# Ternary clipping moved from VectorE to GpSimd, constants of a count in a column of their own, keys spread over more rounds

## The chip, the cores and the metric

The kernel runs on one core of one Trainium2 chip. The metric is the device time of one execution in microseconds. The engines are TensorE (PE, its weight loads PEld), VectorE (DVE), ScalarE (ACT), GpSimd (POOL) and SyncE (SP, which here only starts transfers).

## The reference, cut to what matters

Two layers of a gated cross-attention network run one after the other. The change lies in the first attention and beside it. What is computed there:

```python
sim = einsum('bhnd,bhmd->bnm', Q, K) / (sqrt(d) * H)        # 4 x 512 x 512
topk_vals = top_k(sim, 153)[0]
threshold = topk_vals[:, :, -1:]                            # the 153rd largest of each row
A = sigmoid(sim) * (sim >= threshold)
x = x + tanh(g) * ((1 - gamma) * norm(x) + gamma * (A + A.T) * 0.5)
# the feed-forward behind it takes ternary weights:
wq = clip(round(w / mean(|w|)), -1, 1)
# the second attention needs keys made from the context: k_r = rope(ctx) @ W_kr
```

## The kernel before, in words

The threshold of each of the 2048 rows is found by bisection, without a sort. The rows lie in 16 tiles of 128 rows, and the tiles in two groups of 8 (`g` is 0 or 1). Each group takes 26 steps. A step compares every row's 512 keys (int16 numbers made from `sim`) with the row's present middle, counts those above it, and halves the interval. After 13 steps the keys are made anew at a finer scale (`refine`, line 744). The list `EVENTS` orders the 52 steps as rounds k = 0 to 51: rounds 0 to 3 and then every odd round up to 47 are of group 0, every even round from 4 on and the last four are of group 1, so that one group is counted while the other is marked.

A round goes like this:

- `mark(k)` on VectorE writes marks (0 or 1) for 5 or 6 of the 8 tiles (line 771), and `marks(k)` on ScalarE writes signs for the other 3 or 2 (line 591). In odd rounds from 15 to 41 VectorE has 5 tiles, in all others 6. Both wait for the group's new middles (`mid`). VectorE signals `md`, ScalarE `ma`.
- `total(k)` on TensorE adds the marks up: 32 products with the identity (line 444), each of 8 blocks of 16 columns, collect 128 partial sums (8 tiles by 16) in the group's PSUM bank. Ahead of them stands one product (line 441) that puts the constants `less` under the sums; it waits for VectorE's marks only.
- `count` on VectorE adds each tile's 16 partial sums (line 777) and `halve` makes the new middle (line 782). VectorE does this after the marks of the following round, so its order is mark(k+1), count(k), halve(k), mark(k+2).

Other work is woven into the rounds. After `total(k)`, TensorE makes the products of keys that `keys_made(k)` lists (line 478, an fp32 product of 128 x 512 into banks 2 to 5). VectorE copies a key out two rounds later when the round's number is divisible by 3 (line 867), ScalarE in the other rounds (line 614), and SyncE sends it to memory. ScalarE scales and rounds one of 12 pieces of ternary weights to int16 (`scaled`, line 558) in the rounds `SCALED` = 15, 17, 20, 22, 25, 27, 30, 32, 35, 37, 40, 42. VectorE clips it to -1..1 and writes bf16 (`ternary`, line 759) two rounds later, after that round's marks and the halving. The clipping frees one of three ring buffers; SyncE then loads the next piece (line 377). GpSimd turns the context (`krot`, up to 39 us) and makes the factors `xa` and `xb` (up to 86.5 us); then it has nothing to do until 217.6 us.

The clipping's place in an iteration of VectorE's loop over the rounds:

```python
mark(k)
if held:
    count(*held)
    halve(*held)
    held = None
if k - 2 in SCALED:
    ternary(SCALED.index(k - 2))
```

Of the kernel before, what the change touches and what calls it, by code (L numbers as in the profile page):

```python
# [20 lines left out]
TOPK = 153  # L21
# [6 lines left out]
NW = 12  # L28
# [194 lines left out]
class Front:  # L223


    def __init__(self, M, K):
        self.nm = Norms(M)
        self.ctxt = M.tile([128, 4, S], F32, "ctxt")
        self.wqk = M.tile([128, 2, 128], F32, "wqk")
        self.qt = M.tile([128, 2, S], F32, "QT")  # L230
        self.kt = M.tile([128, 2, S], F32, "KT")
        self.sim = M.tile([128, NT, S], F32, "SIM")
        self.a2 = [M.tile([128, 4, S], F32, "A2")]
        M.top += 8192
        at = M.top
        self.a2.append(M.tile([128, 4, S], F32, "A2b"))
        M.top = at
        self.ring = [M.tile([128, 2048], F32, f"wr{i}") for i in range(3)]
        self.wsum = M.tile([128, NW], F32, "wsum")
        self.wmsum = M.tile([128, 4], F32, "wmsum")  # L240
        self.winv = M.tile([128, 4], F32, "winv")
        self.center = M.tile([128, NT], F32, "center")
        self.unit = M.tile([128, NT], F32, "unit")
        self.shift = M.tile([128, NT], F32, "shift")
        self.base = M.tile([128, NT], F32, "base")
        self.dense = M.tile([128, 2, NT], F32, "dense")
        self.mid = M.tile([128, NT], F32, "mid")
        self.cnt = M.tile([128, NT], F32, "cnt")
        self.cb = M.tile([128, NT], F32, "cb")
        self.xa = M.tile([128, NT], F32, "xa")  # L250
        self.xb = M.tile([128, NT], F32, "xb")
        self.marks = M.tile([128, NT, S], BF16, "marks")
        self.less = M.tile([128, 2, 8, 16], BF16, "less")
        self.stt = M.tile([128, NT, 6], F32, "sst")
        self.smv = M.tile([128, NT, 2], F32, "smv")
        self.sd = M.tile([128, NT], F32, "sd")

        at = M.top
        M.top = M.at["WG"] + 20480
        first = M.tile([128, 4, S], I16, "KEYa")  # L260
        M.top = M.at["WG"] + 28672
        second = M.tile([128, 4, S], I16, "KEYb")
        M.top = M.at["QT"]
        fine = M.tile([128, 8, S], I16, "KEYc")
        M.top = M.at["A2"] + 8192
        self.other = M.tile([128, 8, S], I16, "KEYd")
        M.top = at
        self.coarse, self.fine = (first, second), fine

        M.top = M.at["A2"]  # L270
        self.kvt = M.tile([128, 4, S], F32, "KVT")
        self.kts = M.tile([128, 4, S], F32, "KTS")
        M.top = M.at["WD"]
        self.ktab = M.tile([128, 2, S], F32, "KTAB")
        self.wkr = M.tile([128, NH // 2, 128], F32, "WKR")
        self.kst = M.tile([128, 4, S], F32, "KST")
# [30 lines left out]
SCALED = [15 + 5 * i // 2 for i in range(NW)]  # L307


def on_vector(k):  # L310

    return LEAST if SCALED[0] <= k < SCALED[-1] and k % 2 else LEAST + 1
# [7 lines left out]

def keys_before(k):

    return min(32, max(0, k - KEYS_FROM) + sum(j < k for j in (9, 12, 15, 18)))


def keys_made(k):
# [86 lines left out]
def front_tensor(e, w, K, F0):  # L413
# [22 lines left out]
    def total(k):  # L436

        g, it = EVENTS[k]
        w.wait_ge(S_["less"], 8)
        w.wait_ge(S_[f"md{g}"], it + 1)  # L440
        e.matmul(PS[7 - g][:, 0:128], K.identb[:], F.less[:, on_vector(k) - LEAST].rearrange("p t c -> p (t c)"), start=True, stop=False)
        w.wait_ge(S_[f"ma{g}"], it + 2)
        for c in range(32):
            m = e.matmul(PS[7 - g][:, 0:128], K.identb[:], F.marks[:, 8 * g:8 * g + 8, 16 * c:16 * c + 16], start=False, stop=c == 31)  # L444
        m.then_inc(S_[f"total{g}"].sem, 1)

    def similar(tiles):
# [235 lines left out]
def front_vector(e, w, dc, K, F0):  # L683
# [3 lines left out]
    e.memset(K.magic[:], MAGIC).then_inc(S_["const"].sem, 1)  # L687


    dc.inc(e.memset(F.less[:], 0.0))  # L690
    w.wait_ge(dc.sem, dc.n)
    for i in range(2):
        e.memset(F.less[:, i, 0:LEAST + i, 0], -352.0).then_inc(S_["less"].sem, 1)
        e.memset(F.less[:, i, 0:LEAST + i, 1], 352 - (512 - TOPK + 0.5)).then_inc(S_["less"].sem, 1)
        e.memset(F.less[:, i, LEAST + i:8, 0], -200.0).then_inc(S_["less"].sem, 1)
        e.memset(F.less[:, i, LEAST + i:8, 1], 200 - (512 - 2 * TOPK + 1.5)).then_inc(S_["less"].sem, 1)
    w.wait_ge(S_["d_cst"], 16)
    dc.inc(e.tensor_copy(K.identb[:], K.ident))
    for k in range(4):
# [47 lines left out]
        dc.inc(m)  # L747
        w.wait_ge(dc.sem, dc.n)

    def ternary(i):  # L750

        r = rounded(F, i)
        w.wait_ge(S_["wsc"], i + 1)
        if i >= 8:
            w.wait_ge(S_["kmm"], 32)
            for j in range(4):
                w.wait_ge(S_[f"d_st{j}"], 128)
        w.wait_ge(S_["ma0"], COARSE + 1 if i in (6, 7) else 0)
        e.tensor_scalar(wtile(K, i), r.rearrange("p (a n) -> p a n", a=4) if i >= 8 else r, -1.0, 1.0, ALU.max, ALU.min).then_inc(S_["wq"].sem, 1)

    def mark(k):

        g, it = EVENTS[k]
# [10 lines left out]
    def count(g, it):  # L774
        c = slice(8 * g, 8 * g + 8)
        w.wait_ge(S_[f"total{g}"], it + 1)
        dc.inc(e.tensor_reduce(F.cnt[:, c], PS[7 - g][:, 0:128].rearrange("p (t c) -> p t c", t=8), AX, ALU.add))

    def halve(g, it):
        c = slice(8 * g, 8 * g + 8)  # L780
# [41 lines left out]
    for k, (g, it) in enumerate(EVENTS[:LATE + 4]):  # L822
        mark(k)
        if held:
            count(*held)
            halve(*held)
            held = None
        if k - 2 in SCALED:
            ternary(SCALED.index(k - 2))
        late = k - LATE  # L830
        if k == 0:
            w.wait_ge(S_["gth"], 2)
            dc.inc(e.tensor_scalar(K.cc[:, 2:3], K.gth[:, 0:1], -0.5, 0.5, ALU.mult, ALU.add))
            w.wait_ge(dc.sem, dc.n)
            dc.inc(e.tensor_tensor(K.cc[:, 0:1], K.cc[:, 2:3], K.gth[:, 1:2], ALU.mult))
            dc.inc(e.tensor_scalar(K.cc[:, 3:4], K.gth[:, 0:1], 0.25, 0.25, ALU.mult, ALU.add))
            w.wait_ge(dc.sem, dc.n)
            e.tensor_tensor(K.cc[:, 1:2], K.cc[:, 3:4], K.gth[:, 1:2], ALU.mult).then_inc(S_["cc"].sem, 1)
        elif k == 12:
            w.wait_ge(S_["wabs"], NW)  # L840
            for m in range(3):
                e.tensor_reduce(F.wmsum[:, m:m + 1], F.wsum[:, 4 * m:4 * m + 4], AX, ALU.add).then_inc(S_["wmsum"].sem, 1)
        elif k == 16:
            feed_factors(e, w, dc, K, F0)
        elif k == 14:
            w.wait_ge(S_["wtot"], 1)
            for m in range(3):
                dc.inc(e.tensor_scalar(K.G0[:, m:m + 1], PS[0][:, m:m + 1], 1.0 / (1 << 20), EPS, ALU.mult, ALU.max))
            w.wait_ge(dc.sem, dc.n)
            e.reciprocal(F.winv[:, 0:3], K.G0[:, 0:3]).then_inc(S_["winv"].sem, 1)  # L850
        elif late in (0, 1):
            kept(*range(4 * late, 4 * late + 4))
        elif late == 2:
            back(0, 1, 2, 3)
        elif late == 3:
            feed0_stats(e, w, dc, K, F0)
        if k in ROWS:
            rows(range(2 * ROWS.index(k), 2 * ROWS.index(k) + 2))
        for t in SPREAD.get(k, ()):
            spread(t)  # L860
        if k == LEAD - 1:
            bounds(1)
        for i in keys_out(k) if key_on_vector(k) else ():
            w.wait_ge(S_["kmm"], i + 1)
            w.wait_ge(S_[f"d_st{i % 4}"], 16 * (i // 4))
            w.wait_ge(S_["kev"], i)
            e.tensor_copy(F.kst[:, i % 4], PS[2 + i % 4][:]).then_inc(S_["kev"].sem, 1)
        held = g, it
        if k == len(EVENTS) - 1 or EVENTS[k + 1][0] == g:
            count(g, it)  # L870
            halve(g, it)
            held = None
# [43 lines left out]
def front_gpsimd(e, w, pc, K):  # L916

    S_, F = K.S, K.F
    for b in range(4):
        w.wait_ge(S_["d_ktab"], 16)  # L920
        w.wait_ge(S_[f"d_ctx{b}"], 16)
        w.wait_ge(S_[f"d_kts{b}"], 16)

        w.wait_ge(S_["md0"], 1 if b == 3 else 0)
        e.tensor_tensor(F.kvt[:, b], F.ctxt[:, b], F.ktab[:, 0], ALU.mult)
        w.wait_ge(S_["md0"], 2 if b == 3 else 0)
        pc.inc(e.tensor_tensor(F.kts[:, b], F.kts[:, b], F.ktab[:, 1], ALU.mult))
        w.wait_ge(S_["md0"], 3 if b == 3 else 0)
        w.wait_ge(pc.sem, pc.n)
        e.tensor_tensor(F.kvt[:, b], F.kvt[:, b], F.kts[:, b], ALU.add).then_inc(S_["krot"].sem, 1)  # L930
# [9 lines left out]
    pc.inc(e.tensor_scalar(F.xb[:], F.xb[:], -1.0, None, ALU.mult))  # L940
    w.wait_ge(pc.sem, pc.n)
    e.tensor_scalar(F.xa[:], F.xa[:], 1.0, None, ALU.add).then_inc(S_["cb"].sem, 1)


def front_done(w, K):
# [2365 lines left out]
```

## Time and profile before

| what | us |
|---|---|
| median of 3 runs | 1734.05 (1732.85 to 1735.21) |
| the profiled execution, its own time | 1732.34 |
| its span in the trace | 1730.5 |
| rounds 0 to 51, first mark to last count | 24.0 to 209.4 |

The span is the time between the first and the last instruction of the trace; 1.8 us of the execution lie around it. Durations below are of this one execution. In the timeline a row may merge several instructions of one line that follow each other; the number after x is their count.

### The profile page before, as it was taken

To read this page: it belongs to the slowest core of one execution; us is meant where nothing else is said; L and a number is where in the kernel's file an instruction comes from. 1 tells how busy PE (TensorE), PEld (TensorE's weight loads), DVE (VectorE), ACT (ScalarE), POOL (GpSimd) and SP (SyncE) were. 2 spreads that over 40 slices of the span, in tenths; PEclk is the share of its full clock that TensorE was granted. 3 is DMA by queue.
4 is the path that set the end of the run, shared out by engine and by line. 5 is a ranking of instruction groups with operands and counts; after the bars stand their busy time and mean duration, and the time that the engine had idled before them with its cause. 6 is when DMAs were issued, how large, how long until landed. Compare 5 with 4: busy or idle time off the path is not lost.

```text
span 1730.5 us, 28004 instructions
## 1 busy us (share of the span) xinstructions
PE 1662.8 (96%) x9726; PEld 1174.6 (68%) x9776; DVE 1501.7 (87%) x2933; ACT 1019.8 (59%) x1863; POOL 811.7 (47%) x876
## 2 busy tenths in 40 slices
PE   8798899999998999999999899999999999999999
PEld 5576766666665666676666578778777877874443
DVE  6988889999998899999999887877887888879885
ACT  7888778879996212112111766666666665646664
POOL 3100023121222777666666677667666666755110
PEclk9999999999999999999999999999999999999999
DMA  8764116556751233223333523323223223133444
GB/s 323 265 214 166 38 51 158 125 122 165 163 133 37 74 108 81 82 73 81 81 79 107 174 70 88 88 70 92 77 70 87 81 62 80 50 124 75 92 90 106
DMA packets 157915, 186.05 MB, mean 108 GB/s; under 512 B 85584, under 2 KB 112464, under 8 KB 154576
## 3 DMA queue, kind: packets, MB, share of 16 engines
q1 hardware_dynamic: 146160, 154.58, 32.6%
q10 hardware_dynamic: 11616, 29.70, 6.1%
q8 instruction: 78, 1.28, 0.3%
q14 instruction: 61, 0.50, 0.1%
HBM read 110.83 MB, written 37.75 MB: 86 GB/s over the span
## 4 chain that ended last, share of the span: by engine, by line
PE 69%; DVE 22%; ACT 4%; issue 3%; POOL 1%; DMA 0%; ACTq 0%; DVEq 0%
PE ps L2613 6%; PE ps L2602 5%; PE ps L2103 4%; PE ps L2682 4%; PE ps L2736 3%; PE ps L2738 3%; PE ps L2737 3%; PE ps L444 3%; PE ps L2684 3%; PE ps L2683 3%; PE ps L2058 3%; PE ps L1646 3%; PE ps L1664 3%; PE ps L2060 3%; PE ps L1638 3%
## 5 line engine op out<-in xcount | busy, mean ns | idle before, releaser
L2652 POOL TENSOR_SCALAR E<-E,ri 128x512 f32<-128x512 f32 x250 | 387.0, 1565 | 188.2 <-DVE ri L2636 177.8
L2622 ACT ACTIVATE E<-ps,nm 128x512 f32<-128x512 f32 x256 | 175.5, 691 | 85.4 <-DVE nm L2629 85.4
L2371 POOL TENSOR_TENSOR R<-R,R 128x512 f32<-128x512 f32 x128 | 163.1, 1296 | 115.1 <-DVE R L2312 115.1
L2754 ACT ACTIVATE TH<-ps 128x512 fp32r<-128x512 f32 x256 | 140.0, 602 | 123.3 <-PE ps L2613 123.3
L2823 DVE TENSOR_TENSOR TL<-ps,TH 128x512 fp32r<-128x512 f32 x256 | 165.2, 685 | 29.0 <-ACT TH L2754 28.7
L2191 ACT ACTIVATE KH<-ps 128x512 fp32r<-128x512 f32 x64 | 38.3, 598 | 247.1 <-PE ps L2083 232.3
L2629 DVE TENSOR_REDUCE nm<-ps 128x1 f32<-128x512 f32 x256 | 162.3, 679 | 0.5 <-PE ps L2602 0.4
L1575 POOL TENSOR_SCALAR sc<-sc,gs 128x1 f32<-128x1 f32 x32 | 15.0, 468 | 310.0 <-DVE sc L1447 310.0
L2613 PE MATMUL ps<-CST,E 128*128 128x128 f32 x1024 | 134.2, 273 | 3.0 <-DVE TL L2823 1.5
L2613 PEld LDWEIGHTS ps<-CST,E 128*128 128x128 f32 x1024 | 118.8, 140 | 24.9 <-issue 3.6
L1438 DVE SCALAR_TENSOR_TENSOR U<-fTH,sc,ps 128x512 f32<-128x512 f32 x128 | 95.1, 745 | 27.7 <-PE ps L1646 19.0
L2682 PE MATMUL ps<-TH,VH 128*128 128x512 f32 x256 | 110.9, 433 | 0.0
L2602 PE MATMUL ps<-KP,QR 64*128 64x512 f32 x384 | 106.4, 409 | 2.5 <-DVE R L2313 2.5
L444 PE MATMUL ps<-marks,identb 128*128 128x128 bf16 x1664 | 105.9, 224 | 2.1 <-ACT marks L591 1.8
L2602 PE MATMUL ps<-KS,QR 64*128 64x512 f32 x384 | 106.5, 409 | 0.0
L444 PEld LDWEIGHTS ps<-marks,identb 128*128 128x128 bf16 x1664 | 99.3, 101 | 9.3 <-issue 5.4
L2058 PE MATMUL ps<-HH,WQH 128*128 128x512 f32 x256 | 103.8, 405 | 0.0
L2684 PE MATMUL ps<-TH,VL 128*128 128x512 f32 x256 | 101.3, 396 | 0.0
L2736 PE MATMUL ps<-MH,CH 128*128 128x512 f32 x256 | 100.2, 391 | 0.8 <-DVE X L2832 0.8
L2683 PE MATMUL ps<-TL,VH 128*128 128x512 f32 x256 | 100.6, 393 | 0.0
L2060 PE MATMUL ps<-HH,WQL 128*128 128x512 f32 x256 | 100.1, 391 | 0.0
L2738 PE MATMUL ps<-MH,CL 128*128 128x512 f32 x256 | 99.9, 390 | 0.0
(294 smaller groups left out, 4515.7 us busy)
## 6 DMA issues: line engine op xcount, KB each, us to landing
wr<-in_wff SPq DMA_DIRECT2D x24, 1024.0 KB, 5.4
aw<-in_wff ACTq DMA_DIRECT2D x40, 512.0 KB, 4.8
scratch<-QS SPq DMA_DIRECT2D x128, 128.0 KB, 2.4
KS<-KP SPq DMA_DIRECT2D x64, 256.0 KB, 3.6
QR<-scratch SPq DMA_DIRECT2D x64, 256.0 KB, 3.4
keys<-KST SPq DMA_DIRECT2D x32, 256.0 KB, 3.2
KR<-keys SPq DMA_DIRECT2D x30, 256.0 KB, 3.8
wscr<-awb ACTq DMA_DIRECT2D x24, 256.0 KB, 3.4
```

Of the source, the lines that this page charges most:

```text
L444: m = e.matmul(PS[7 - g][:, 0:128], K.identb[:], F.marks[:, 8 * g:8 * g + 8, 16 * c:16 * c + 16], start=False, stop=c == 31)
L2058: e.matmul(key_bank(K, n)[:], wh, Q.hh[:, b, k, :], start=k == 0, stop=False)
L2371: e.tensor_tensor(Q.r1[:, z, c, :], Q.r1[:, z, c, :], ask_r2(Q, n)[:, c, :], ALU.add).then_inc(S_["radd"].sem, 1)
L2602: m = e.matmul(K.PS[2 * z + u][:], queries(A, n)[r, a, c], k[u][r, p % 2, b, :], start=i == 0, stop=i == 2)
L2613: m = e.transpose(K.PS[4 + x % 2][:, 128 * c:128 * c + 128], A.e[:, x % EB, 128 * c:128 * c + 128], K.ident)
L2622: e.activation(A.e[:, x % EB, :], K.PS[x % 4][:], ACT.Exp, bias=A.nm[:, c], accum_out=A.sm[:, c]).then_inc(S_["exp"].sem, 1)
L2629: e.tensor_reduce(A.nm[:, c], K.PS[x % 4][:], AX, ALU.max, negate=True).then_inc(S_["mx"].sem, 1)
L2652: e.tensor_scalar(A.e[:, x % EB, :], A.e[:, x % EB, :], A.ri[:, x % 8:x % 8 + 1], None, ALU.mult).then_inc(K.S["pl"].sem, 1)
L2682: e.matmul(PS[6][:], vh, A.th[:, n % 2, c, :], start=c == 0, stop=False)
L2683: e.matmul(PS[6][:], vh, A.tl[n % 2][:, c, :], start=False, stop=False)
L2684: m = e.matmul(PS[6][:], vl, A.th[:, n % 2, c, :], start=False, stop=c == 3)
L2823: e.tensor_tensor(A.tl[n % 2][:, :, c], PS[4 + x % 2][:].rearrange("p (c n) -> p c n", c=4), A.th[:, n % 2, :, c].bitcast(F32), ALU.subtra ...
```

## The change

- The constants leave the 128 partial sums. Each tile's sums now have 17 columns in PSUM (`counts`, 8 blocks at a pitch of 17): 16 for the marks and one for the constants. Two products of 8 columns write the constant column in a group's first round and again when the number of VectorE's tiles differs from the round two before; the 32 products of marks overwrite their own 16 columns each round. `count` adds 17 columns. A clearing of `less` at the start goes.
- The keys: exactly one product of keys a round, in rounds 4 to 35. Before, rounds 9, 12, 15 and 18 made two, and the last was in round 31.
- The clipping moves from VectorE's rounds to GpSimd, all 12 behind `xa`. GpSimd starts each as soon as ScalarE has rounded the piece and the place of its output is free. The two bounds are applied in the other order.

```diff
--- before.py
+++ after.py
@@ -250,7 +250,7 @@
         self.xa = M.tile([128, NT], F32, "xa")
         self.xb = M.tile([128, NT], F32, "xb")
         self.marks = M.tile([128, NT, S], BF16, "marks")
-        self.less = M.tile([128, 2, 8, 16], BF16, "less")
+        self.less = M.tile([128, 2, 2, 8], BF16, "less")
         self.stt = M.tile([128, NT, 6], F32, "sst")
         self.smv = M.tile([128, NT, 2], F32, "smv")
         self.sd = M.tile([128, NT], F32, "sd")
@@ -307,6 +307,11 @@
 SCALED = [15 + 5 * i // 2 for i in range(NW)]
 
 
+def counts(K, g):
+
+    return K.PS[7 - g][:, 0:136].rearrange("p (t c) -> p t c", t=8)
+
+
 def on_vector(k):
 
     return LEAST if SCALED[0] <= k < SCALED[-1] and k % 2 else LEAST + 1
@@ -320,7 +325,7 @@
 
 def keys_before(k):
 
-    return min(32, max(0, k - KEYS_FROM) + sum(j < k for j in (9, 12, 15, 18)))
+    return min(32, max(0, k - KEYS_FROM))
 
 
 def keys_made(k):
@@ -438,10 +443,12 @@
         g, it = EVENTS[k]
         w.wait_ge(S_["less"], 8)
         w.wait_ge(S_[f"md{g}"], it + 1)
-        e.matmul(PS[7 - g][:, 0:128], K.identb[:], F.less[:, on_vector(k) - LEAST].rearrange("p t c -> p (t c)"), start=True, stop=False)
+        if it == 0 or on_vector(k) != on_vector(k - 2):
+            for i in range(2):
+                e.matmul(counts(K, g)[:, :, 16], K.identb[:], F.less[:, on_vector(k) - LEAST, i], start=i == 0, stop=i == 1)
         w.wait_ge(S_[f"ma{g}"], it + 2)
         for c in range(32):
-            m = e.matmul(PS[7 - g][:, 0:128], K.identb[:], F.marks[:, 8 * g:8 * g + 8, 16 * c:16 * c + 16], start=False, stop=c == 31)
+            m = e.matmul(counts(K, g)[:, :, 0:16], K.identb[:], F.marks[:, 8 * g:8 * g + 8, 16 * c:16 * c + 16], start=c == 0, stop=c == 31)
         m.then_inc(S_[f"total{g}"].sem, 1)
 
     def similar(tiles):
@@ -687,13 +694,11 @@
     e.memset(K.magic[:], MAGIC).then_inc(S_["const"].sem, 1)
 
 
-    dc.inc(e.memset(F.less[:], 0.0))
-    w.wait_ge(dc.sem, dc.n)
     for i in range(2):
-        e.memset(F.less[:, i, 0:LEAST + i, 0], -352.0).then_inc(S_["less"].sem, 1)
-        e.memset(F.less[:, i, 0:LEAST + i, 1], 352 - (512 - TOPK + 0.5)).then_inc(S_["less"].sem, 1)
-        e.memset(F.less[:, i, LEAST + i:8, 0], -200.0).then_inc(S_["less"].sem, 1)
-        e.memset(F.less[:, i, LEAST + i:8, 1], 200 - (512 - 2 * TOPK + 1.5)).then_inc(S_["less"].sem, 1)
+        e.memset(F.less[:, i, 0, 0:LEAST + i], -352.0).then_inc(S_["less"].sem, 1)
+        e.memset(F.less[:, i, 1, 0:LEAST + i], 352 - (512 - TOPK + 0.5)).then_inc(S_["less"].sem, 1)
+        e.memset(F.less[:, i, 0, LEAST + i:8], -200.0).then_inc(S_["less"].sem, 1)
+        e.memset(F.less[:, i, 1, LEAST + i:8], 200 - (512 - 2 * TOPK + 1.5)).then_inc(S_["less"].sem, 1)
     w.wait_ge(S_["d_cst"], 16)
     dc.inc(e.tensor_copy(K.identb[:], K.ident))
     for k in range(4):
@@ -747,17 +752,6 @@
         dc.inc(m)
         w.wait_ge(dc.sem, dc.n)
 
-    def ternary(i):
-
-        r = rounded(F, i)
-        w.wait_ge(S_["wsc"], i + 1)
-        if i >= 8:
-            w.wait_ge(S_["kmm"], 32)
-            for j in range(4):
-                w.wait_ge(S_[f"d_st{j}"], 128)
-        w.wait_ge(S_["ma0"], COARSE + 1 if i in (6, 7) else 0)
-        e.tensor_scalar(wtile(K, i), r.rearrange("p (a n) -> p a n", a=4) if i >= 8 else r, -1.0, 1.0, ALU.max, ALU.min).then_inc(S_["wq"].sem, 1)
-
     def mark(k):
 
         g, it = EVENTS[k]
@@ -774,7 +768,7 @@
     def count(g, it):
         c = slice(8 * g, 8 * g + 8)
         w.wait_ge(S_[f"total{g}"], it + 1)
-        dc.inc(e.tensor_reduce(F.cnt[:, c], PS[7 - g][:, 0:128].rearrange("p (t c) -> p t c", t=8), AX, ALU.add))
+        dc.inc(e.tensor_reduce(F.cnt[:, c], counts(K, g), AX, ALU.add))
 
     def halve(g, it):
         c = slice(8 * g, 8 * g + 8)
@@ -825,8 +819,6 @@
             count(*held)
             halve(*held)
             held = None
-        if k - 2 in SCALED:
-            ternary(SCALED.index(k - 2))
         late = k - LATE
         if k == 0:
             w.wait_ge(S_["gth"], 2)
@@ -916,6 +908,21 @@
 def front_gpsimd(e, w, pc, K):
 
     S_, F = K.S, K.F
+
+    def ternary(i):
+
+        r = rounded(F, i)
+        w.wait_ge(S_["wsc"], i + 1)
+        if i == 8:
+            w.wait_ge(S_["krot"], 4)
+        elif i > 8:
+            w.wait_ge(S_["kmm"], 32)
+        if i > 9:
+            for j in range(4):
+                w.wait_ge(S_[f"d_st{j}"], 128)
+        w.wait_ge(S_["ma0"], COARSE + 1 if i in (6, 7) else 0)
+        e.tensor_scalar(wtile(K, i), r.rearrange("p (a n) -> p a n", a=4) if i >= 8 else r, 1.0, -1.0, ALU.min, ALU.max).then_inc(S_["wq"].sem, 1)
+
     for b in range(4):
         w.wait_ge(S_["d_ktab"], 16)
         w.wait_ge(S_[f"d_ctx{b}"], 16)
@@ -940,6 +947,8 @@
     pc.inc(e.tensor_scalar(F.xb[:], F.xb[:], -1.0, None, ALU.mult))
     w.wait_ge(pc.sem, pc.n)
     e.tensor_scalar(F.xa[:], F.xa[:], 1.0, None, ALU.add).then_inc(S_["cb"].sem, 1)
+    for i in range(NW):
+        ternary(i)
 
 
 def front_done(w, K):
```

## Rows read from the trace of the kernel before

**Rows 1.** Page, part 1: busy us (share), instructions.
```profile
PE 1662.8 (96%) x9726; PEld 1174.6 (68%) x9776; DVE 1501.7 (87%) x2933; ACT 1019.8 (59%) x1863; POOL 811.7 (47%) x876
```

**Rows 2.** Busy time in stretches: us, PE, PEld, DVE, ACT, POOL, PEclk, DMA, GB/s.
```profile
84.00:112.00 28.00, 28.00 (x336) 21.45 (x335) 22.85 (x96) 26.25 (x35) 1.99 (x7) 1.00 0.72 250
...
152.00:183.00 31.00, 25.17 (x409) 23.17 (x407) 28.10 (x112) 25.82 (x33) 0.00 (x0) 1.00 0.33 116
```

**Rows 3.** Waits, 84 to 183 us: us in total, times, longest.
```profile
DVE cnt L777 <- PE ps L444: 12.5, 18, 1.6
```

**Rows 4.** Counts of VectorE, 84 to 183 us: ns min/median/max, starts.
```profile
L777 DVE TENSOR_REDUCE cnt<-ps x33: 279/291/293, 83.8 to 182.8; 128x8 f32<-128x128 f32 x33
```

**Rows 5.** Timeline, 92 to 100 us: start, us, engine, line, operation.
```profile
92.15 1.94 PE L478 MATMUL ps<-KVT,WKR 128*128 128x512 f32 x4
92.33 0.57 ACT L614 ACTIVATE KST<-ps 128x512 f32<-128x512 f32 x1
...
96.37 0.69 DVE L759 TENSOR_SCALAR WG<-wr 128x2048 bf16<-128x2048 int16 x1
...
96.68 0.22 PE L441 MATMUL ps<-less,identb 128*128 128x128 bf16 x1
...
96.73 1.95 PE L444 MATMUL ps<-marks,identb 128*128 128x128 bf16 x32
96.97 0.35 DVE L771 TENSOR_SCALAR marks<-KEYd,mid 128x512 bf16<-128x512 int16 x1
...
97.31 1.40 DVE L771 TENSOR_SCALAR marks<-KEYd,mid 128x512 bf16<-128x512 int16 x5
...
98.52 1.08 PE L478 MATMUL ps<-KVT,WKR 128*128 128x512 f32 x2
```

**Rows 6.** Timeline, 157 to 161 us.
```profile
157.40 1.99 ACT L558 ACTIVATE wr<-wr,winv 128x2048 int16<-128x2048 f32 x1
157.41 0.28 DVE L777 TENSOR_REDUCE cnt<-ps 128x8 f32<-128x128 f32 x1
...
157.93 0.35 DVE L771 TENSOR_SCALAR marks<-KEYd,mid 128x512 bf16<-128x512 int16 x1
...
159.30 1.32 ACT L591 ACTIVATE marks<-KEYd,mid 128x512 bf16<-128x512 int16 x2
...
160.67 1.96 PE L444 MATMUL ps<-marks,identb 128*128 128x128 bf16 x32 [0.71 <-ACT marks L591]
```

**Rows 7.** Timeline, 19 to 29 us, VectorE beside GpSimd.
```profile
19.62 1.26 POOL L930 TENSOR_TENSOR KVT<-KVT,KTS 128x512 f32<-128x512 f32 x1
...
27.98 1.11 DVE L838 TENSOR_TENSOR cc<-cc,gth 128x1 f32<-128x1 f32 x1
```

**Rows 8.** VectorE's line 717: ns min/median/max, first and last start.
```profile
L717 DVE TENSOR_SCALAR sd<-smv x2: 172/628/1083, 19.8 to 43.5; 128x8 f32<-128x8 f32 x2
```

**Rows 9.** Timeline, 79 to 84 us, marks beside small GpSimd work.
```profile
79.50 1.47 DVE L771 TENSOR_SCALAR marks<-KEYd,mid 128x512 bf16<-128x512 int16 x5
...
80.31 0.22 POOL L111 TENSOR_TENSOR bna<-bna,bnve 128x16 f32<-128x16 f32 x1
...
82.61 1.32 POOL L109 TENSOR_TENSOR bna<-bnr 128x16 f32<-128x16 f32 x1
...
83.25 0.60 DVE L771 TENSOR_SCALAR marks<-KEYb,mid 128x512 bf16<-128x512 int16 x2
```

**Rows 10.** GpSimd's groups by shape: busy us, mean ns, idle before.
```profile
L2652 POOL TENSOR_SCALAR E<-E,ri 128x512 f32<-128x512 f32 x250 | 387.0, 1565 | 188.2 <-DVE ri L2636 177.8 <-ACT E L2645 10.4
...
L113 POOL TENSOR_SCALAR G<-G 128x4 f32<-128x4 f32 x12 | 2.4, 199 | 1.0
...
L113 POOL TENSOR_SCALAR bna<-bna 128x16 f32<-128x16 f32 x3 | 0.6, 205 | 0.3
...
L942 POOL TENSOR_SCALAR xa<-xa 128x16 f32<-128x16 f32 x1 | 0.3, 270 | 0.1
```

**Rows 11.** Timeline, 117 us: a count after a pause of TensorE.
```profile
117.50 3.62 PE L444 MATMUL ps<-marks,identb 128*128 128x128 bf16 x32
```

## The prediction

> **What bounds the kernel now.** I read the page's busy times first. TensorE is busy for 96% of the span and VectorE for 87% [rows 1], but that is a mean over stages, and this change touches only the rounds, 24 to 209 us. So I read the busy times of stretches. From 84 to 112 us TensorE is busy without a gap and VectorE for 22.85 of 28 us; from 152 to 183 us TensorE has 25.17 of 31 us and VectorE 28.10 [rows 2]. So two regimes follow each other. While keys are made TensorE sets the pace, and when the keys are done VectorE (with ScalarE) does.
>
> The waits between 84 and 183 us say how often. 33 counts start there [rows 4], and before 18 of them VectorE stood still for TensorE's sums, 12.5 us in all or 0.69 us each [rows 3]. Those 0.69 us are slack of VectorE. The other 15 were late through VectorE or ScalarE themselves. ScalarE's signs in their turn wait for the new middles, so whatever delays VectorE's halving delays ScalarE.
>
> The timeline shows a round of each kind. At 96.73 us a count begins on TensorE (1.95 us), and one key follows at 98.52. Round 15 has two keys: x4 records in 1.94 us against x2 in 1.08, so one key costs TensorE 0.86 us [rows 5]. At 157.40 us ScalarE rounds a piece for 1.99 us, its signs of the next round come at 159.30 for 1.32, and TensorE's sums start only behind them at 160.67 [rows 6]. There ScalarE binds, and work taken from VectorE gives nothing.
>
> **The constants.** Each round loses one product of 128 columns of the 33. A round's 32 take 1.95 us and one alone (line 441) 0.22, so they follow each other at (1.95 - 0.22)/31 = 0.056 us [rows 5]. Where VectorE is late nothing hides it either, since the product stands between the last mark and the sums. I take 30 rounds by 0.056 = -1.7 us, bounds 0 and 52 x 0.056 = -2.9. The products of constants that remain (two in each of four rounds) and 8 more columns a count are not in the trace; below nothing they can't be, and from the 0.056 us of a 16 times wider product they are under 0.5 us together. I take +0.2. The clearing at the start lies before the first DMA has landed and costs nothing.
>
> **The keys.** Three doubles (rounds 12, 15, 18) lie where TensorE sets the pace: 3 x 0.86 = -2.6 us. Round 9's lies where VectorE is late. The four go to rounds 32 to 35, where TensorE has some room and ScalarE has little. I charge 0.86 once for TensorE there, and ScalarE copies three of these four keys, 0.57 us each [rows 5], in rounds 34, 35 and 37, next to its roundings; half of 1.7 is on the path. Sum -2.6 + 0.9 + 0.8 = -0.9 us; bounds -2.6 and +0.8. SyncE's four later stores of keys are read only in a much later stage.
>
> **The clip off VectorE.** It starts at 96.37 us and takes 0.69, and the next mark begins at 96.97, 0.60 behind its start [rows 5]. Two of the 12 lie beside the remaking of keys, where VectorE alone is at work: 2 x 0.60. Of the other ten, four are followed by a wait for TensorE or lie where ScalarE binds as at 160.67, and give nothing. Six I count at half, 0.3. Sum -3.0 us; bounds 0 and 12 x 0.60 = -7.2.
>
> **The clip on GpSimd** is not in the trace. Two numbers are wanted: its length, and what it does to VectorE.
>
> Length: multiplying 128 x 512 by a number per row takes GpSimd 1565 ns [rows 10], or 2.67 ns an element over a base of 0.2, which makes 0.2 + 2048 x 2.67 = 5.7 us. But that row and line 942 (270 ns for 16 elements) have one operation and none behind it. Line 113 has two operations with constants, as the clip has. It takes 199 ns for 4 elements and 205 for 16 [rows 10], 0.5 ns an element, or 1.2 us for 2048. The clip is nearest to line 113 in form. Such small rows show little of a slope, so I take twice theirs, 1 ns: 2.2 us, of which some 2.0 behind the start-up of 0.2. Bounds 1.2 and 5.7.
>
> Effect: at 19.62 us GpSimd works for 1.26 us, and a VectorE instruction that starts at 19.8 takes 1.083, to the end of GpSimd's, where its twin at 43.5 takes 0.172 [rows 7, 8]. L838 takes 1.11 us for one column beside GpSimd's next run [rows 7]. So some instructions of VectorE stand still while GpSimd works. Are the marks among them? At 82.61 a GpSimd instruction of 16 columns takes 1.32 us instead of 0.2 and ends when the run of marks ends (83.25 + 0.60) [rows 9]. At 79.50 five marks take 1.47 us instead of the 1.40 of another round [rows 5], beside GpSimd instructions of 0.22 us that were not held up [rows 9]. So marks and GpSimd do exclude each other, and GpSimd can slip in between two marks. The first row speaks for an exclusion for a whole instruction, the second for one that costs only what is really moved.
>
> The Trainium skill has a rule here (SBUF — State Buffer, Who interferes with whom): VectorE's two-port modes, which tensor_scalar enters, and GpSimd share one pair of ports, and whoever is first keeps it for its whole instruction. By it the sum would be the one I make below; by the row at 79.50 alone the clips would cost nothing, and the change would save 5.4 us. The Trainium skill's GPSIMD Engine Reference, 4.1 Engine selection, calls one-input work there roughly line-rate; at 1 element a cycle of its 1.2 GHz that is an estimate of 1.7 us for 2048, which the 1565 ns for 512 contradict and line 113 does not.
>
> I take the whole instruction, because L717 and L838 waited for all of it. A clip starts when ScalarE's rounding ends, at any point of VectorE's round. If it slips in between marks, the marks end 2.0 us later. If it waits for the end of the marks, 0.52 us of counting and halving would have passed anyway (from the count at 157.41 to the marks at 157.93, 0.52) [rows 6], though the halving itself reads two tensors like L838 and waits; then the next marks are 1.5 us late. Mean 1.74. Six clips (after the roundings of rounds 15, 17, 20, 25, 32 and 40) fall where TensorE sets the pace and 0.69 us is free: 6 x 1.05 = 6.3. Six fall where nothing is free: 6 x 1.74 = 10.4. Sum +16.7 us. With 1.0 in place of 2.0 it is 6 x 0.04 + 6 x 0.73 = +4.6; with 5.5 it is 6 x 4.54 + 6 x 5.23 = +58.6. Behind the delayed marks stand TensorE's sums, the count, and ScalarE's signs. GpSimd itself delays nobody: its next work is at 217 us, and a clip of 2.2 us ends before VectorE's did (two rounds later), so the ring loads come earlier, not later.
>
> **Sum.** -1.7 + 0.2 - 0.9 - 3.0 + 16.7 = +11.3 us. The stage behind the rounds starts from the last count, so it moves as a whole. The profiled execution took 1732.34 us (span 1730.5 and 1.8 around it), which makes 1743.6. It lies 1.7 us below the median of the runs, so for the median I add to 1734.05: 1745.4 us. A difference under 0.2%, 3.5 us, can't be told from none here.
>
> **Rivals.**
> - *The clips cost VectorE nothing* (the row at 79.50, for example because GpSimd takes its ports piece by piece): -5.4 us, 1728.7, faster. Against it stand L717 and L838. The turning point is 5.4/12 = 0.45 us of delay per clip. Chance 0.24.
> - *Short holds*: a clip of 1.2 us. -5.4 + 4.6 = -0.8, 1733.3, no change. Chance 0.12 with what lies around it.
> - *A slow clip*, 5.7 us, as line 2652's rate has it: -5.4 + 58.6 = +53 us. TensorE then stands still for some 4 us each time, and at 117.50, after such a pause, 32 products took 3.62 us instead of 1.95 [rows 11]: up to 12 x 1.67 = 20 us more. 1787 to 1807. For it: the only long tensor_scalar rows of GpSimd. Chance 0.14.
> - *Sums at a pitch of 17 columns slow TensorE down.* No row has such an output. With 1/8 more a product, 32 x 0.007 = 0.22 us a round; over 50 rounds +11 us, on top. The nearest row for an upper bound is a key's 0.86 us for 2 x 512 columns, 0.84 ns a column against 0.44 now: 1.6 us in each of the 35 or so rounds where TensorE is the pace or nearly, +57 us. The Trainium skill (PSUM — Partial Sum Buffer, Specifications (TRN2)) says that any non-contiguous access slows matmuls significantly, without a figure. The marks are read in blocks of 16 already, without harm. Chance that this decides: 0.06.
>
> **How the numbers follow.** The forecast case has the remaining 0.44, with its own range of 1738 to 1763 (clip of 1.4 to 3.7 us). The likeliest time is 1745.4. The range must reach to the faster rival and leave out the slow clip: 1728 to 1772. Faster 0.24, same 0.12, slower 0.64.
>
> **What would show it.** Right: in the rounds from 15 on, marks (line 771) or halvings beside a GpSimd clip of 2 us or more have maxima of 1 to 2 us instead of the 0.35 at 96.97, the waits of TensorE for marks grow, and a round with a clip is about 1.4 us longer. A round paced by TensorE should get 0.056 us shorter, and rounds 12, 15 and 18 by 0.86. Wrong: marks of 0.35 us beside the clips (the faster rival), a clip far from 2.2 us, or spacings of marks' products above 0.056 us.

## Result and the profile after

The changed kernel takes 1744.93 us (median of 6 runs, 1742.15 to 1746.65), the kernel before in the same series 1734.34 us (1732.69 to 1735.47). The ratio is 1.0058, 95% interval 1.0048 to 1.0069: slower, by some 10 us. The forecast was 1745.4 us. The profiled execution took 1742.8 us, with a span of 1741.0, or 10.5 us more than before.

The page, part 1, busy us of each engine, as in [rows 1]:

```profile
PE 1668.1 (96%) x9682; PEld 1179.0 (68%) x9732; DVE 1514.1 (87%) x2921; ACT 1018.9 (59%) x1862; POOL 834.3 (48%) x888
```

GpSimd has 22.6 us and 12 instructions more. VectorE lost 12 clips and its busy time still rose by 12.4 us. The busy times of stretches answer to [rows 2] (us, PE, PEld, DVE, ACT, POOL, PEclk, DMA, GB/s):

```profile
84.00:112.00 28.00, 26.73 (x328) 20.87 (x327) 25.28 (x95) 24.56 (x32) 7.67 (x10) 1.00 0.62 210
152.00:183.00 31.00, 25.88 (x361) 21.97 (x360) 28.94 (x94) 26.00 (x34) 7.85 (x5) 1.00 0.43 149
```

From 84 to 112 us TensorE no longer works without a gap, and VectorE went from 22.85 to 25.28 us. From 152 to 183 us VectorE is busy for 28.94 us with 94 instructions where it had 28.10 with 112: fewer instructions, each longer. Which ones is seen in VectorE's groups by shape from 84 to 193 us (busy us, mean ns of one | idle before). First the kernel before:

```profile
L771 DVE TENSOR_SCALAR marks<-KEYd,mid 128x512 bf16<-128x512 int16 x108 | 31.3, 349 | 0.3
...
L771 DVE TENSOR_SCALAR marks<-KEYc,mid 128x512 bf16<-128x512 int16 x68 | 19.9, 348 | 0.2
...
L782 DVE SCALAR_TENSOR_TENSOR mid<-cnt,base 128x8 f32<-128x8 f32 x36 | 6.0, 167 | 1.2
L759 DVE TENSOR_SCALAR WG<-wr 128x2048 bf16<-128x2048 int16 x8 | 5.5, 689 | 0.1
...
L744 DVE TENSOR_SCALAR KEYc<-SIM,center,dense 128x512 int16<-128x512 f32 x8 | 3.7, 546 | 0.1
```

And the changed kernel:

```profile
L765 DVE TENSOR_SCALAR marks<-KEYd,mid 128x512 bf16<-128x512 int16 x102 | 34.5, 397 | 0.5
L765 DVE TENSOR_SCALAR marks<-KEYc,mid 128x512 bf16<-128x512 int16 x64 | 23.7, 424 | 0.4
L776 DVE SCALAR_TENSOR_TENSOR mid<-cnt,base 128x8 f32<-128x8 f32 x34 | 11.1, 326 | 1.2
...
L749 DVE TENSOR_SCALAR KEYc<-SIM,center,dense 128x512 int16<-128x512 f32 x8 | 5.3, 734 | 0.1
```

Count times rise of the mean: 102 x 0.048 + 64 x 0.076 + 34 x 0.159 + 8 x 0.188 = 16.7 us, or 1.4 us for each of the 12 clips. I call this sum the hold. The twelve clips that left VectorE were worth 12 x 0.69 = 8.3 us of its time. The medians did not move; single instructions did. Duration by line (ns min/median/max), 84 to 193 us, of the marks, the halving, the clip and TensorE's sums:

```profile
L765 DVE TENSOR_SCALAR marks<-KEYd,mid x102: 337/347/2045, 84.3 to 191.4; 128x512 bf16<-128x512 int16 x102
...
L776 DVE SCALAR_TENSOR_TENSOR mid<-cnt,base x34: 166/168/1795, 84.1 to 192.3; 128x8 f32<-128x8 f32 x34
...
L924 POOL TENSOR_SCALAR WG<-wr x8: 1892/1892/2076, 90.5 to 152.7; 128x2048 bf16<-128x2048 int16 x8
...
L451 PE MATMUL ps<-marks,identb x1065: 219/226/327, 84.0 to 193.0; 128*128 128x128 bf16 x178
```

The same line of marks had a maximum of 383 ns before, the halving 169. The clip takes 1892 ns. And TensorE's product of marks has a median of 226 ns; before it was 219 (the line stands under the experiment with a pitch of 18). The timeline from 90 us on shows single cases (start, us, engine, line), beside [rows 5]:

```profile
90.27 3.09 DVE L765 TENSOR_SCALAR marks<-KEYd,mid 128x512 bf16<-128x512 int16 x5
...
90.54 1.89 POOL L924 TENSOR_SCALAR WG<-wr 128x2048 bf16<-128x2048 int16 x1 [4.00 <-ACT wr L565]
...
93.42 2.07 PE L451 MATMUL ps<-marks,identb 128*128 128x128 bf16 x32 [0.81 <-DVE marks L765]
...
96.23 2.06 PE L451 MATMUL ps<-marks,identb 128*128 128x128 bf16 x32
...
98.21 1.89 POOL L924 TENSOR_SCALAR WG<-wr 128x2048 bf16<-128x2048 int16 x1 [5.78 <-ACT wr L565]
...
98.66 1.46 DVE L776 SCALAR_TENSOR_TENSOR mid<-cnt,base 128x8 f32<-128x8 f32 x1
```

Five marks take 3.09 us in place of 1.40, since a clip begins at 90.54 behind the first of them; TensorE's sums then wait. At 98.66 the halving ends at 100.12, with the clip (98.21 + 1.89 = 100.10). That is what L717 and L838 did in [rows 7, 8]. The waits of the changed kernel, 84 to 193 us (us in total, times, longest), answer to [rows 3], which end at 183:

```profile
ACT marks L598 <- DVE mid L776: 23.1, 20, 2.8
...
PEld ps L451 <- DVE marks L765: 20.3, 14, 5.3
PE ps L451 <- DVE marks L765: 12.8, 6, 4.5
...
DVE cnt L771 <- PE ps L451: 7.7, 13, 1.6
```

In the same 84 to 193 us of the kernel before, VectorE waits for TensorE 20 times, 13.1 us in all, where it now does so 13 times and for 7.7 us. TensorE's waits for VectorE's marks grow from 10.7 us to 14.6 (the 12.8 above and 1.8 of line 448). The last count of the 52 starts 7.1 us later. First the kernel before, then the changed one (ns min/median/max, first and last start):

```profile
L777 DVE TENSOR_REDUCE cnt<-ps x52: 258/291/293, 30.6 to 209.1; 128x8 f32<-128x128 f32 x52
```
```profile
L771 DVE TENSOR_REDUCE cnt<-ps x52: 267/299/301, 30.4 to 216.2; 128x8 f32<-128x136 f32 x52
```

So 7.1 of the 10.5 us arise in the rounds. Another 1.8 arise directly behind them: the feed-forward's first product with the weights WG (line 1195 before, 1204 after; below the first gate product) starts at 222.9 and 231.9 us, 9.0 us apart. There the first products of the feed-forward ran at a lower granted clock. The stretches from 210 us on, first of the kernel before:

```profile
210.00:222.00 12.00, 6.70 (x28) 4.72 (x27) 8.49 (x23) 7.42 (x12) 0.59 (x2) 0.87 0.07 27
222.00:234.00 12.00, 11.93 (x57) 6.29 (x58) 9.66 (x18) 9.47 (x16) 0.57 (x2) 0.99 0.00 1
```

and of the changed kernel:

```profile
210.00:222.00 12.00, 8.87 (x68) 5.88 (x66) 9.86 (x35) 7.78 (x14) 0.00 (x0) 0.95 0.13 44
222.00:234.00 12.00, 9.82 (x34) 6.59 (x34) 6.64 (x12) 7.07 (x11) 0.59 (x2) 0.62 0.00 0
```

The same work lies 7 us later in the changed kernel, so the four rows have to be read together. At the lower of the two clock levels (1.2 GHz, a clock of 0.5) TensorE spent some 3.4 of the 24 us before, and 10.3 of them after. The remainder, 1.5 us, comes in later stages, which the change doesn't touch. Some of it may be the clock again: from 960 to 980 us the granted clock is 0.91 in the changed kernel's execution and 1.00 in the other.

### The profile page after: what moved, and what is told of

Its sections match the earlier page's. It is cut to its first block, busy times and chain, and to the rows that moved or that the text cites. A ratio compares the mean times of both kernels' runs of the same rounds, so it can differ in the third digit from the quotient of the medians.

```text
span 1741.0 us, 27965 instructions
## 1 busy us (share of the span) xinstructions
PE 1668.1 (96%) x9682; PEld 1179.0 (68%) x9732; DVE 1514.1 (87%) x2921; ACT 1018.9 (59%) x1862; POOL 834.3 (48%) x888
## 4 chain that ended last, share of the span: by engine, by line
PE 67%; DVE 23%; ACT 4%; issue 3%; POOL 1%; DMA 0%; ACTq 0%; SPq 0%; DVEq 0%
PE ps L2622 6%; PE ps L2611 5%; PE ps L2112 4%; PE ps L2691 4%; PE ps L2745 3%; PE ps L2747 3%; PE ps L2746 3%; PE ps L451 3%; PE ps L2693 3%; PE ps L2692 3%; PE ps L1655 3%; PE ps L1673 3%; PE ps L2067 3%; PE ps L1647 3%; PE ps L2069 3%
## 5 line engine op out<-in xcount | busy, mean ns | idle before, releaser
L2661 POOL TENSOR_SCALAR E<-E,ri 128x512 f32<-128x512 f32 x250 | 387.0, 1565 | 188.9 <-DVE ri L2645 177.8
L2380 POOL TENSOR_TENSOR R<-R,R 128x512 f32<-128x512 f32 x128 | 162.5, 1292 | 117.3 <-DVE R L2321 117.3
L451 PEld LDWEIGHTS ps<-marks,identb 128*128 128x128 bf16 x1664 | 104.4, 103 | 52.7 <-DVE marks L765 40.0
L451 PE MATMUL ps<-marks,identb 128*128 128x128 bf16 x1664 | 111.7, 231 | 26.2 <-DVE marks L765 21.3
```

What stands on the lines that cost most here:

```text
L451: m = e.matmul(counts(K, g)[:, :, 0:16], K.identb[:], F.marks[:, 8 * g:8 * g + 8, 16 * c:16 * c + 16], start=c == 0, stop=c == 31)
L2380: e.tensor_tensor(Q.r1[:, z, c, :], Q.r1[:, z, c, :], ask_r2(Q, n)[:, c, :], ALU.add).then_inc(S_["radd"].sem, 1)
L2661: e.tensor_scalar(A.e[:, x % EB, :], A.e[:, x % EB, :], A.ri[:, x % 8:x % 8 + 1], None, ALU.mult).then_inc(K.S["pl"].sem, 1)
```

## Experiments

Executions of one kernel differ in their mean granted clock, and the time goes with it: over all executions of this study a fit gives 1.06 us for 0.001 of mean clock. The last column is each kernel's time by that fit at a clock of 0.993, where the kernel before has 1733.3 ± 0.4. It is a help against the scatter and no more: where an edit itself makes TensorE pause and its clock fall, that column takes part of the edit's own cost away. The kernel before ran again beside each group of experiments: its median is 1733.46 beside the first four and 1731.92 beside the others.

| kernel | median us | ratio to before, 95% | last count starts | at equal clock |
|---|---|---|---|---|
| changed | 1744.93 | 1.0058 [1.0048, 1.0069] | 216.2 | 1742.7 ± 1.1 |
| clip only | 1741.10 | 1.0054 [1.0039, 1.0068] | 216.7 | 1741.4 ± 1.0 |
| constants only | 1737.83 | 1.0032 [1.0017, 1.0047] | 209.4 | 1737.1 ± 1.0 |
| keys only | 1734.82 | 1.0008 [0.9996, 1.0020] | 211.0 | 1734.0 ± 0.7 |
| all but the clip | 1738.38 | 1.0037 [1.0023, 1.0050] | 211.8 | 1735.9 ± 0.9 |
| constants, column outer | 2003.59 | 1.1562 [1.1546, 1.1578] | | |
| constants, pitch 18 | 1733.31 | 1.0005 [0.9996, 1.0014] | 204.4 | 1733.6 ± 0.8 |
| changed, clip twice | 1766.34 | 1.0197 [1.0181, 1.0212] | 243.1 | 1760.4 ± 1.6 |
| changed, clip in four | 1737.71 | 1.0032 [1.0019, 1.0044] | 210.3 | 1737.4 ± 1.1 |

The last count is that of one profiled execution each. How much of a difference there is the edit's own is seen where it arises. The start of some counts, read from the timelines, in us; for all but the first column, the difference to it:

| | before | clip only | constants | pitch 18 | keys only | all but clip | changed | in four |
|---|---|---|---|---|---|---|---|---|
| round 0 | 30.6 | -0.9 | -0.4 | -0.5 | +0.2 | -1.0 | -0.2 | -0.3 |
| round 22 | 117.3 | +1.6 | +0.7 | -1.2 | -2.2 | -3.1 | +0.8 | -0.7 |
| round 25 | 127.8 | +2.1 | -0.3 | -4.2 | -2.0 | -4.3 | -0.2 | -3.3 |
| round 36 | 162.7 | +5.0 | -0.2 | -4.5 | -1.4 | -2.1 | +4.0 | -0.5 |
| round 38 | 167.7 | +5.8 | -0.2 | -4.5 | +2.0 | +2.3 | +4.9 | 0.0 |
| round 51 | 209.1 | +7.6 | +0.4 | -4.7 | +2.0 | +2.8 | +7.1 | +1.2 |
| first gate product | 222.9 | +7.4 | +2.9 | -3.3 | +2.9 | +5.3 | +9.0 | +1.4 |
| granted clock, 112 to 137 us | 0.86 | 0.86 | 0.93 | 1.00 | 0.86 | 0.93 | 0.93 | 1.00 |

Between rounds 22 and 25 the difference follows the last row and not the edit: at a clock of 0.86 it moves by 0.5 us at most, at 0.93 by -1.0 to -1.2, at 1.00 by -2.6 and -3.0. So up to 3 us of a last count can be this alone.

**Clip only.** The kernel before, with `ternary` and its 12 calls on GpSimd as in the change.

```diff
-        if k - 2 in SCALED:
-            ternary(SCALED.index(k - 2))
+    for i in range(NW):      # in front_gpsimd, behind xa
+        ternary(i)
```

> The kernel before with the clipping alone moved to GpSimd. Theory A (a clip of 1.9 us keeps VectorE's marks and halvings out for its whole length): 12 holds of some 1.7 us less the free time where TensorE sets the pace, less 3 us of clipping that leaves VectorE: +9 to +14 us against before, nearly the whole effect of the change, with marks of up to 1.9 us in the trace. Theory B (the sums at a pitch of 17 columns, 2.06 us instead of 1.95 a round, carry the loss): below +5 us.

Measured 1.0054, most of the whole change's loss. The hold, summed as above over all of VectorE's groups, is 18.1 us here (16.8 in the changed kernel). 18.1 less the 8.3 us of the clips taken away is 9.8; the time rose by 8.1 ± 1.1. That is 1 to 1.5 us below what theory A expected and well above theory B. So the free clip is out: GpSimd holds VectorE, and most of the hold reaches the end.

**Constants only.** `counts`, the column of constants, `less` and the count of 17 columns as in the change; clips and keys as before.

```diff
-    return K.PS[7 - g][:, 0:128]
+    return K.PS[7 - g][:, 0:136].rearrange("p (t c) -> p t c", t=8)
```

> The kernel before with the constants alone in a column of their own (pitch of 17). Theory A: a round paced by TensorE gains 0.056 us by the missing product and loses 0.11 by slower ones, so 0 to +3 us against before. Theory B: +5 us or more.

Measured 1.0032, slower, where the prediction had a gain of 1.5 us. The 32 products of marks take 2.06 us instead of 1.95: (2.06 - 1.95) = 0.11 us more a round against 0.056 us for the product that fell away. The time lies between the two theories' ranges, and 33 to 50 rounds of the difference of 0.055 us are only 1.8 to 2.8 us.

**Keys only.**

```diff
-    return min(32, max(0, k - KEYS_FROM) + sum(j < k for j in (9, 12, 15, 18)))
+    return min(32, max(0, k - KEYS_FROM))
```

> The kernel before with one product of keys in each of rounds 4 to 35 alone. The prediction's term: -0.9 us, bounds -2.6 and +0.8. A rival: the four late keys meet ScalarE's roundings and the change is +1 us or more.

Measured 1.0008, no difference that can be told, where -0.9 was forecast. The timeline of this kernel shows a wait that the prediction lacked:

```profile
163.84 0.69 DVE L759 TENSOR_SCALAR WD<-wr 128x2048 bf16<-128x2048 int16 x1 [2.04 <-DMA keys<-KST]
...
166.24 0.29 PE L441 MATMUL ps<-less,identb 128*128 128x128 bf16 x1 [3.11 <-DVE marks L771]
...
166.32 3.27 PE L444 MATMUL ps<-marks,identb 128*128 128x128 bf16 x32
```

The last four clips write where the keys' staging lies, so `ternary` waits for all 32 keys and the landing of their stores. With keys up to round 35 the ninth clip stands still for that store for 2.04 us on VectorE, with the marks of the round queued behind it, and TensorE waits 3.11 us. Behind that pause its 32 products take 3.27 us instead of 1.95; from 166 to 170 us its granted clock is 0.62. By the table above the whole costs 3.4 us (from -1.4 in round 36 to +2.0 in round 38), after the keys had gained 2.4 us up to round 22.

**All but the clip.** Constants and keys as in the change, clips on VectorE.

```diff
-    for i in range(NW):      # GpSimd, of the changed kernel
-        ternary(i)
+        if k - 2 in SCALED:  # VectorE, as before
+            ternary(SCALED.index(k - 2))
```

> The changed kernel with the clipping back on VectorE, so constants and keys together. Theory A: -2 to +2 us against before. Theory B: +5 us or more. If the parts add up, it is the sum of the two runs with one part each.

Measured 1.0037, between the two theories' ranges as it stands (4.9 us). At equal clock it is 6.8 ± 1.4 us below the changed kernel: that is the clip's share when the rest is in place. The kernel is 2.6 us above the kernel before at equal clock, where the two parts sum to 3.8 + 0.7 = 4.5. The wait for the keys' store is here too, in the waits of VectorE from 150 to 200 us:

```profile
DVE cnt L782 <- PE ps L451: 5.1, 8, 2.0
DVE WD L764 <- DMA keys<-KST: 2.6, 1, 2.6
```

In the changed kernel VectorE has no such line, and GpSimd's clips wait only for ScalarE's rounding.

**Constants, column outer.** To make TensorE's output contiguous again, column c of tile t at 8c + t; TensorE then reads the marks with 512 elements between neighbours.

```diff
-            m = e.matmul(counts(K, g)[:, :, 0:16], K.identb[:], F.marks[:, 8 * g:8 * g + 8, 16 * c:16 * c + 16], ...
+            m = e.matmul(counts(K, g)[:, 0:16, :], K.identb[:], F.marks[:, 8 * g:8 * g + 8, 16 * c:16 * c + 16].rearrange("p t c -> p c t"), ...
```

> The constants-only kernel, but with the 17 columns of a tile strewn (column c of tile t at 8c + t), so that a product writes 128 neighbouring PSUM columns and reads its marks at a large step instead. If the pitch of 17 in PSUM is what made 32 products take 2.06 us in place of 1.95, they take 1.95 again and a round paced by TensorE gains 0.056 us: 0 to -2 us against before at an equal clock. If the gaps are innocent, or reading at a step is the slower side, products take 2.06 us or more and the kernel is +3 us or more.

Measured 1.156. TensorE is busy for all of 92 to 152 us at a granted clock of 0.54, and 32 products take 7.18 us, 3.7 times the 1.95. The clock accounts for a factor of up to 1.9, so the read accounts for another 2 or so. It says nothing on the output's pitch; for that it was the wrong experiment, since it moved the step to the side where it costs far more. Why the clock stays low while TensorE is busy throughout is open.

**Constants, pitch 18.** The blocks of sums 18 columns apart, an even number; the count reads 17 of them.

```diff
-    return K.PS[7 - g][:, 0:136].rearrange("p (t c) -> p t c", t=8)
+    return K.PS[7 - g][:, 0:144].rearrange("p (t c) -> p t c", t=8)
...
-        dc.inc(e.tensor_reduce(F.cnt[:, c], counts(K, g), AX, ALU.add))
+        dc.inc(e.tensor_reduce(F.cnt[:, c], counts(K, g)[:, :, 0:17], AX, ALU.add))
```

> The constants-only kernel with a pitch of 18 columns in place of 17 (every tile's sums begin on an even column). If an odd start is what slows the products, they fall back to 1.95 us for 32 and the kernel is 3 to 4 us faster than constants-only. If any gap in the output costs, they stay at 2.06 and the time too.

Measured 1.0005: the loss is gone, 3.5 ± 1.3 us at equal clock. The product of marks by line (ns min/median/max), 84 to 193 us, first before, then pitch 17 (constants only), then pitch 18:

```profile
L444 PE MATMUL ps<-marks,identb x1137: 217/219/314, 84.8 to 193.0; 128*128 128x128 bf16 x190
```
```profile
L451 PE MATMUL ps<-marks,identb x1132: 219/226/327, 84.6 to 192.9; 128*128 128x128 bf16 x189
```
```profile
L451 PE MATMUL ps<-marks,identb x1175: 216/219/315, 84.0 to 193.0; 128*128 128x128 bf16 x196
```

At a pitch of 18 the output has gaps too, so gaps as such cost nothing. What costs is the pitch of 17, at which every second block starts on an odd column; no other odd pitch was measured. In the rounds the two profiled executions part by 5.1 us (+0.4 and -4.7), of which 2.0 arise between rounds 22 and 25 with the clock; the other 3 us are near the 3.6 that 33 rounds of 0.11 us make.

Against the kernel before, pitch 18 gains 4.7 us in the rounds, of which 3.0 go with the clock and 0.5 are there at round 0. That leaves 1.2 us for the product of constants that fell away. At the end no gain is seen: 1733.6 ± 0.8 against 1733.3.

**Changed, clip twice.** Each clip of the changed kernel is done twice, the second behind the first.

```diff
-        e.tensor_scalar(wtile(K, i), ..., 1.0, -1.0, ALU.min, ALU.max).then_inc(S_["wq"].sem, 1)
+        for again in range(2):
+            m = e.tensor_scalar(wtile(K, i), ..., 1.0, -1.0, ALU.min, ALU.max)
+            if again == 0:
+                pc.inc(m)
+                w.wait_ge(pc.sem, pc.n)
+        m.then_inc(S_["wq"].sem, 1)
```

> The changed kernel with each clip on GpSimd made twice. Theory A (a clip holds VectorE's marks and halvings for its length): another 12 x 1.9 us of holds, of which half to all reach the end: +11 to +22 us against the changed kernel. Theory C (what costs is the hand-over and not the length): under +4 us.

Measured 1.0197: 17.7 ± 1.9 us above the changed kernel at equal clock, for 12 clips more, or 1.5 us each, within the range of theory A. As it stands the difference is 21.4 us, or 1.8 us each; all four executions have a clock of 0.987, the lowest mean of all kernels here but for the column outer, so part of the clock's share is likely caused by the holds. The maxima stay at one clip's length, since a VectorE instruction waits for one GpSimd instruction and then gets its turn (marks by line, 84 to 193 us):

```profile
L765 DVE TENSOR_SCALAR marks<-KEYd,mid x78: 335/346/2055, 84.8 to 190.0; 128x512 bf16<-128x512 int16 x78
```

So each further clip costs about as much as the mean hold of 1.4 to 1.5 us: little of it was covered by slack.

**Changed, clip in four.** The same elements in four instructions of 512 columns.

```diff
+        for j in range(4):
+            to = wtile(K, i)[:, j, :] if i >= 8 else wtile(K, i)[:, 512 * j:512 * j + 512]
+            m = e.tensor_scalar(to, r[:, 512 * j:512 * j + 512], 1.0, -1.0, ALU.min, ALU.max)
+        m.then_inc(S_["wq"].sem, 1)
```

> The changed kernel with each clip cut into four instructions of 512 columns. Theory A, with a hold for each whole instruction: marks get a turn between the pieces and no mark or halving is longer than about 1 us, but the held time is the same or more, so -3 to +3 us against the changed kernel. If instead only one long hold hurts and short ones are hidden, it gives back 5 us or more.

Measured 1.0032, 5.3 ± 1.6 us less than the changed kernel at equal clock. By line, a piece and the marks:

```profile
L926 POOL TENSOR_SCALAR WG<-wr x32: 609/647/815, 90.4 to 150.2; 128x512 bf16<-128x512 int16 x32
...
L765 DVE TENSOR_SCALAR marks<-KEYc,mid x68: 339/347/787, 115.2 to 188.0; 128x512 bf16<-128x512 int16 x68
```

and the timeline beside the first clip:

```profile
90.15 2.46 DVE L765 TENSOR_SCALAR marks<-KEYd,mid 128x512 bf16<-128x512 int16 x5
...
90.42 2.65 POOL L926 TENSOR_SCALAR WG<-wr 128x512 bf16<-128x512 int16 x4 [4.93 <-ACT wr L565]
```

The longest mark is 0.79 us instead of 2.05, and five marks take 2.46 us instead of 3.09: the engines take turns, piece by piece. The hold, over all groups, sums to 11.9 us, 4.9 less than in the changed kernel, and the time fell by 5.3. The expectation missed this: it held the sum of the holds for unchanged, and gave 3 us at most. It is not free either: at equal clock the clip in four on GpSimd is still 1.5 ± 1.4 us above the same kernel with its clips on VectorE (1737.4 against 1735.9).

Without a measurement are the changed kernel with pitch 18, alone and together with the clip in four; products without use in TensorE's pauses at 210 to 220 us, to see what the lower clock behind the rounds costs; and six tiles of marks on VectorE in every round. So that hold and pitch together are the whole loss is not shown.

## Why the prediction was right in its total, and where its terms were not

**The hold: right.** The instruction taken as the model, with two operations and constants, was the right one: 1892 ns against 2.2 us forecast, 0.9 ns an element against the 1.0 taken. Marks and halving stand still for a whole GpSimd instruction, which decided between the two readings of [rows 7 to 9]. The mean hold was forecast at 1.74 us for a 2.0 us clip and is 1.4 to 1.5. The whole-instruction rule of the Trainium skill (SBUF — State Buffer, Who interferes with whom) agrees with the 2045 ns mark and the 787 ns mark beside pieces. Clip free, short and slow clip are ruled out.

**The clip's net price: too high.** The step "The clip off VectorE" counted six clips at half, -3.0 us, and the effect on GpSimd was +16.7: +13.7 net. Measured are +8.1 ± 1.1 (alone) and +6.8 ± 1.4 (on top of the rest). Both halves of the net were off. The forecast had 12 x 1.74 = 20.9 us of hold, measured are 16.8 to 18.1, so 3 to 4 us too much. Against it the forecast set 4.1 us of slack and 3.0 us for the clips taken away, 7.1 in all; between the hold of 18.1 us and the 8.1 us that the clip alone cost lie 10.0. The clips taken away are worth 8.3 us at most, so the likely fault is the count of six clips at half and four at nothing. The prediction let work taken from VectorE give nothing where ScalarE binds. But ScalarE's signs in their turn waited for VectorE's halving in the kernel before (84 to 183 us):

```profile
ACT marks L591 <- DVE mid L782: 14.8, 15, 2.6
```

How the 10 us divide between clips taken away and slack was not measured.

**The constants: wrong in sign.** The step took 30 x 0.056 = 1.7 us gained and put the pitch at a chance of 0.06. Measured +3.8 ± 1.1 us at equal clock, and the pitch is the cause: a pitch of 18 takes it back. The rival was right in its place and too high in its size: 0.11 us a round, not 0.22. The prediction's own sign for it came: the products of marks follow each other at (2.06 - 0.23)/31 = 0.059 us, above its 0.056, and a round paced by TensorE got 0.055 us longer, not shorter. Shown are the 0.11 us of TensorE and the loss of time; their way to the end is not fully seen. In the profiled execution with the constants alone the last count is only 0.3 us late. Some 2.5 us arose directly behind it (+2.9 at the first gate product), where the granted clock was low:

```profile
210.00:222.00 12.00, 6.92 (x25) 4.58 (x24) 6.78 (x20) 5.41 (x10) 0.59 (x2) 0.66 0.11 36
222.00:234.00 12.00, 11.75 (x44) 6.45 (x45) 8.02 (x15) 8.01 (x14) 0.56 (x2) 0.77 0.01 1
```

In the kernel before the two stretches have 0.87 and 0.99. TensorE worked for 6.92 of the first 12 us here and for 6.70 before, so its busy time alone doesn't tell why. The profiled execution ends 8.6 us behind the one before, so more than half of that lies in later stages, which the edit doesn't touch; it is one of the slower executions of its kernel (1740.95 us, median 1737.83).

**The keys: right in its terms, one wait missed.** Alone +0.7 ± 0.9 us against -0.9. The doubles taken out gained 2.4 us up to round 22, forecast were 2.6, and rounds 32 to 36 took 0.7 back. The 2.04 us in which the ninth clip waits on VectorE for the store of keys, and the slower products behind that pause, 3.4 us together, were not in the sum, which had said that SyncE's later stores are read only in a much later stage. They are, but the clip waits for them too. In the changed kernel the clip is on GpSimd and this wait is gone. +0.7 less the 2.04 or the 3.4 us is -1.3 or -2.7; the forecast was -0.9 with a bound at -2.6.

**Parts and whole.** At equal clock the parts sum to 8.1 + 3.8 + 0.7 = 12.6 us, the whole is 9.4 ± 1.2. The keys' wait of 2.0 to 2.6 us, gone in the changed kernel, may be most of that difference. It may not be all: constants and keys together, with the wait still there, already lie 1.9 us below the sum of the two. The uncertainty of such differences is about 2 us, so neither is shown.

**The total** came out 0.5 us from the forecast by luck: the clip's net was some 6 us too dear, constants and keys some 7 us too cheap, and the whole is 3 us less than the parts. The direction was not luck, since the hold is the largest term and was read rightly. Of the 10 us some 2 arose behind the rounds from the clock, of which the prediction says nothing. Why the clock is low there in one kernel and not in another is open.

## What to carry to other kernels

Work given to GpSimd beside a VectorE near its limit costs VectorE a large part of each GpSimd instruction's length (1.4 to 1.5 of 1.9 us here), so 0.69 us saved against a 1.9 us instruction is a loss. If such work has to be there, shorter instructions cost less (four of 0.65 us gave 5.3 us back), though here VectorE was still the better place. When a layout in PSUM gains a column, look at the duration of every product that writes it, and try another pitch; here 18 in place of 17 took the loss back. When work is moved later, list every instruction that waits for its transfers: here the clip, not the reader of the keys, was the first. And do not compare two profiled executions by their ends alone: find where the difference arises, and look at the granted clock there.

## What the runs showed of the hardware

- A bf16 product of 128 columns in blocks of 16 takes 226 ns at a pitch of 17 fp32 columns in PSUM and 219 ns at 16 or 18; 32 of them take 2.06 and 1.95 us.
- Read with 512 bf16 elements between neighbours, 32 such products take 7.18 us at a granted clock of 0.54.
- GpSimd's tensor_scalar with two constants, int16 to bf16, takes 1892 ns for 2048 columns and 647 ns for 512 beside a busy VectorE, though a one-operation tensor_scalar by a number per row in fp32 takes 1565 ns for 512 [rows 10].
- VectorE's marks and GpSimd's instructions take turns, one whole instruction each: a second clip right behind the first leaves the longest mark at 2.05 us. A halving of 128 x 8 is held as well, 1795 ns in place of 168.
- Behind a pause of 3.11 us, 32 products of marks took 3.27 us instead of 1.95, at a granted clock of 0.62 from 166 to 170 us (keys only).
